# Ranks in the lists of a graph network's first GAT pass, later tables in rank order, and layer ends worked off by groups of 14 blocks

## What is computed

```python
h = jnp.maximum(_layernorm(x, axis=-1), 0.0)
x = x + _L0_gnn_ref(h, src, dst, 12500)                 # cosine attention over src
h = jnp.maximum(_layernorm(x, axis=-1), 0.0)
x = x + _L1_gnn_ref(h, edge_index, ...)                 # two GATs, each: segment softmax, bias, norm, ELU
h = jnp.maximum(_layernorm(x, axis=-1), 0.0)
x = x + _L2_gnn_ref(h, edge_index, W, b)                # GCN: D^-1/2 A D^-1/2 (h W) + b, ReLU
h = jnp.maximum(_layernorm(x, axis=-1), 0.0)
x = x + _L3_gnn_ref(h, r, a, Wa_w, ..., src, dst, edge_type_4)   # gates and attention by edge type
```

## Time and profile before

| | |
|---|---|
| median of 3 runs | 14001.26 us (13983.39 to 14005.41) |
| the profiled execution: its time, its span | 13982.26 us, 13980.5 us |
| POOL busy | 9215.6 us (66%), 9579 instructions |
| DVE busy | 6105.5 us (44%) |
| ACT, PE busy | 1970.1 us (14%), 1991.1 us (14%) |
| DMA, mean over the span | 43 GB/s |

### The profile page before, as it was taken

One profiled execution on the slowest core, in us unless ns is written; L12 is line 12 of the kernel. 1 busy time (PEld: TensorE's weight loads), 2 busy tenths in 40 slices (PEclk: granted clock), 3 DMA queues, 4 the chain that ended last, 5 costly groups with the idle time before them and its releaser, 6 DMA issues. The chain is left out here.

```text
span 13980.5 us, 109214 instructions
## 1 busy us (share of the span) xinstructions
PE 1991.1 (14%) x7172; PEld 1317.2 (9%) x7172; DVE 6105.5 (44%) x20057; ACT 1970.1 (14%) x6083; POOL 9215.6 (66%) x9579
## 2 busy tenths in 40 slices
PE   8720000000010000001000000100000053333334
PEld 6620000000000000001000000000000032222223
DVE  9981233333333333344333334411111157777775
ACT  0000000010011111101000000100000034444443
POOL 0026576776757777775777777477777747777775
PEclk9755555555555555555555555555555555555555
DMA  0001233334211111111111111011111144444442
GB/s 10 0 27 25 34 27 27 28 28 27 27 22 30 30 30 30 30 29 20 28 28 27 28 28 27 16 27 27 27 27 27 26 177 108 107 108 107 107 104 64
DMA packets 971030, 594.72 MB, mean 43 GB/s; under 512 B 713282, under 2 KB 815699, under 8 KB 970561
## 3 DMA queue, kind: packets, MB, share of 16 engines
q0 software_dynamic: 338528, 472.50, 19.1%
q1 hardware_dynamic: 632411, 121.34, 4.9%
HBM read 507.46 MB, written 85.57 MB: 42 GB/s over the span
## 5 line engine op out<-in xcount | busy, mean ns | idle before, releaser
L926 POOL DMA_INDIRECT got<-gat_tab,list x3472 | 3283.3, 946 | 1116.4 <-issue 1006.8
L926 POOL DMA_INDIRECT got<-rel_tab,list x1736 | 1741.0, 1003 | 644.0 <-issue 472.3
L926 POOL DMA_INDIRECT got<-h_tab,list x1736 | 1661.1, 957 | 713.6 <-issue 519.4
L926 POOL DMA_INDIRECT got<-gcn_tab,list x1736 | 1637.6, 943 | 555.0 <-issue 523.0
L1310 DVE COPY e<-top 128x4 f32 (+1 forms) x920 | 149.5, 163 | 2617.9 <-DMA got<-gat_tab,list 2060.1
L1213 PE MATMUL p_t<-ident,staged 128*128 128x128 f32 x147 | 69.4, 472 | 7277.3 <-ACT staged L1229 7266.4
L1416 DVE TENSOR_REDUCE chunk_sum<-got 128x64 f32<-128x256 f32 (+1 forms) x460 | 253.4, 551 | 1771.0 <-DMA got<-gcn_tab,list 1724.9
L1012 DVE TENSOR_TENSOR prod<-got,h 128x256 f32<-128x256 f32 (+1 forms) x460 | 190.1, 413 | 1402.2 <-DMA got<-h_tab,list 1302.3
L1380 ACT ACTIVATE p<-e 128x20 f32<-128x20 f32 (+3 forms) x920 | 195.6, 213 | 4104.2 <-DVE e L1329 3572.0
L533 POOL DMA_INDIRECT info_tab<-info,rank_i x98 | 125.1, 1277 | 976.7 <-DVEq L511 947.1
L1981 PE MATMUL p_gate<-got,ident 128*128 128x256 f32 (+1 forms) x920 | 539.5, 689 | 1483.0 <-DVE gate L1818 1482.4
(11 more groups left out here) (353 smaller groups left out, 7994.4 us busy)
## 6 DMA issues: line engine op xcount, KB each, us to landing
own<-own_tab SPq DMA_DIRECT2D x460, 160.5 KB, 2.4
got<-gat_tab,list POOLq DMA_INDIRECT x3472
got<-h_tab,list POOLq DMA_INDIRECT x1736
got<-gcn_tab,list POOLq DMA_INDIRECT x1736
got<-rel_tab,list POOLq DMA_INDIRECT x1736
own_tab<-own SPq DMA_DIRECT2D x98, 160.5 KB, 2.6
list<-chunks_dst SPq DMA_DIRECT2D x612, 4.0 KB
chunks_src<-rows_src SPq DMA_DIRECT2D x505, 4.5 KB
```

What stands on the lines that cost most here:

```text
L926: pool.indirect_dma_start(r.got[:, q, j, :], None, table, at(r.lists[s][:, c, j:j + 1]))\
```

## The change

The first table is still written by node number. Its rows grow from 72 to 77 values: own scores, and as the last one four times the row's rank (`number_rows` fills it). In the first GAT pass (`relabel`), which loads all columns of the lists, DVE builds from each gathered row's last value the chunk's list anew (`ranks`): ranks, and ranks times four plus type. ACT writes the turn's four new lists to a second list table, `chunks_rank`, with one DMA, and DVE's next turn waits for that DMA. All later passes read `chunks_rank`, and so their tables can lie in rank order and are written with plain DMAs.

The part of two slots now runs ahead of the part of four in the two GAT and the GCN passes. In the part of four, DVE's and ACT's loops over turns are cut at the ends of seven groups of 14 blocks (the ends are in the new row 9 of `row_i`). After the turns of group g, DVE runs `close(g)`: what `gat_close`, `open_layer` and `gcn_close` did, on 14 blocks (896 columns). After the turns of group g + 1 it takes TensorE's products of group g (`finish(g)`), and ACT writes them to the next table; after the last group nothing lies in between. In the GCN pass TensorE and ACT make the rows of `rel_tab` and `own_tab` of a group from its `close` on, 14 blocks one after the other: three matmuls of 321 columns for each block (the third adds the bias), four activations and two DMAs. SP's loop and POOL's loop over the turns stay whole. The whole-layer stages between these passes are gone, but for the first `project_and_spread` and `gat_open`; `gcn_norm` runs ahead of the first GAT, and the tables' last 128 rows (for empty slots) are written in `load_weights`.

```diff
-def load_lists(nc, sp, lists, part, r, i):
+def load_lists(nc, sp, lists, part, r, i, tab, columns):
...
+def group_turns(eng, lists, g):
+    return (eng.value_load(lists.row_i[0:1, 9, bass.ds(g, 1)], min_val=0, max_val=CHUNKS // RING - 2),
+            eng.value_load(lists.row_i[0:1, 9, bass.ds(g + 1, 1)], min_val=1, max_val=CHUNKS // RING - 2))
...
+                def ranks(q):
+                    chunk = r.lists[q // PER_STAGE][:, q % PER_STAGE, :]
+                    if q == 0:
+                        dve.wait_ge(again_out, i * 16 + 16)
+                    ts.add(nc.vector.scalar_tensor_tensor(out=type_of[:, :], in0=chunk[:, 0:S], scalar=-4.0,
+                                                          in1=chunk[:, SLOTS:SLOTS + S], op0=ALU.mult, op1=ALU.add))
+                    ts.add(nc.vector.tensor_scalar(again[:, q, 0:S], r.got[:, q, :, RW - 1], 0.25, None, ALU.mult))
+                    ts.wait()
+                    dve.sem_inc(r.list_used[q // PER_STAGE], 1)
+                    ts.add(nc.vector.tensor_tensor(again[:, q, SLOTS:SLOTS + S], r.got[:, q, :, RW - 1], type_of[:, :],
+                                                   ALU.add))
...
+            def close(g):
+                blocks = bass.ds(g * GROUP, GROUP)
...
+                ch.link(tt(Y[:, :, :], Y[:, :, :], vec(after.bias), ALU.add))
...
+                dve.wait_ge(std_ready, g * NORMS + 1)
...
+                tt(Y[:, :, :], Y[:, :, :], vec(after.shift), ALU.add).then_inc(y_ready, 1)
+                dve.wait_ge(ex_ready, g + 1)
...
+            def group(g):
+                t0, t1 = group_turns(dve, lists, g)
+                one_block(nc, dve)
+                with dve.Fori(t0, t1) as i:
+                    turn(i)
+
+            group(0)
+            close(0)
+            with dve.Fori(1, TURNS) as g:
+                group(g)
+                finish(g - 1)
+                close(g)
+            finish(TURNS - 1)
...
+                if relabel:
+                    act.wait_ge(e_ready, i * RING + RING)
+                    act.dma_start(k.rank_tab[bass.ds(i * RING + part.base, RING), :, 0:SLOTS + S]
+                                  .rearrange("a p c -> p a c"), again[:, :, :]).then_inc(again_out, 16)
...
+            def store(g):
+                blocks = bass.ds(g * GROUP, GROUP)
+                act.wait_ge(finished, g + 1)
+                act.sem_inc(r.tick, 1)
+                act.dma_start(by_rank(after.table)[:, blocks, :], after.state[:, blocks, 0:after.columns])\
+                    .then_inc(stored, 16)
...
-def gcn_edges(nc, k, part, state, table):
+def gcn_edges(nc, k, part, state, table, after):
...
+                    for j in range(GROUP):
...
+                        act.wait_ge(made, g * GROUP + j + 1)
+                        act.wait_ge(out[w], g * 64 + (32 * (j // HELD) + 32))
...
+                        act.dma_start(by_rank(k.rel_tab)[:, blk, :], rows[w][:, :, :].rearrange("p t c -> p (t c)")
+                                      .unsqueeze(1)).then_inc(out[w], 16)
+                        act.dma_start(k.own_tab[blk].rearrange("a p c -> p (a c)"), own[w][:, :]).then_inc(out[w], 16)
...
-def gat_close(nc, k, heads, c, state, bias, gain, shift, y, x_add):
...
-def gcn_close(nc, k, state, dis, bias, x):
...
-def rel_tables(nc, k, h):
...
+    short_first = PARTS[::-1]
```

More of the change, by code:

```diff
@@ L876, in _, with ring_buffers @@
                 dve.wait_ge(copied[j], TURNS * len(parts))
-def ring_buffers(m, part, width, stages=STAGES):
+def ring_buffers(m, part, width, stages=STAGES, columns=None):
     S = part.slots
@@ L883, in ring_buffers @@
     r.per_stage = RING // stages
-    r.lists = [m.sb(f"list{s}", [P, r.per_stage, S], I32) for s in range(stages)]
+    r.columns = columns or S
+    r.lists = [m.sb(f"list{s}", [P, r.per_stage, r.columns], I32) for s in range(stages)]
     r.meta = m.sb("meta", [1, RING], I32)
@@ L992, in _ @@
                 with sp.Fori(0, n) as i:
-                    load_lists(nc, sp, lists, part, r, i)
+                    load_lists(nc, sp, lists, part, r, i, lists.chunk_tab, part.slots)
         @block.gpsimd
@@ L1272, in gat_edges @@
     S = part.slots
+    lists = k.at_dst
     with ExitStack() as ctx:
         m = Mem(nc, ctx)
-        r = ring_buffers(m, part, W)
+        RW = table.shape[1]
+        r = ring_buffers(m, part, RW, columns=SLOTS + S if relabel else S)
         e = m.sb("e", [P, 2, S + 1, heads])
@@ new lines, in finish @@
+            def finish(g):
+                blocks = bass.ds(g * GROUP, GROUP)
+                dve.sem_clear(close_step)
+                ch = Chain(dve, close_step)
+                dve.wait_ge(made, g + 1)
+                after.rows(dve, ch, blocks, p_o[:, :, 0:GROUP // 2, 0:after.wide].rearrange("p y j w -> p j y w"))
+                dve.sem_inc(finished, 1)
+            if not after:
+                one_block(nc, dve)
+                with dve.Fori(0, n) as i:
+                    turn(i)
+                return
@@ L1377, in _, with turn @@
-            with act.Fori(0, n) as i:
+            n = turns(act, lists, part)
+            def turn(i):
                 for q in range(RING):
@@ new lines, in store, with group @@
+            def store(g):
+                blocks = bass.ds(g * GROUP, GROUP)
+                act.wait_ge(finished, g + 1)
+                act.sem_inc(r.tick, 1)
+                act.dma_start(by_rank(after.table)[:, blocks, :], after.state[:, blocks, 0:after.columns])\
+                    .then_inc(stored, 16)
+            if not after:
+                one_block(nc, act)
+                with act.Fori(0, n) as i:
+                    turn(i)
+            else:
+                def group(g):
+                    t0, t1 = group_turns(act, lists, g)
+                    with act.Fori(t0, t1) as i:
+                        turn(i)
+                group(0)
+                close(0)
+                with act.Fori(1, TURNS) as g:
+                    group(g)
+                    close(g)
+                    store(g - 1)
+                store(TURNS - 1)
+                act.wait_ge(stored, 16 * TURNS)
@@ L1418, in _, with close @@
                     dve.sem_inc(r.got_free[q], 1)
-                    ts.link(nc.vector.tensor_tensor(own, own, chunk_sum[:, :], ALU.add))
+                    ts.link(nc.vector.tensor_tensor(own_row, own_row, chunk_sum[:, :], ALU.add))
+            if not after:
+                one_block(nc, dve)
+                with dve.Fori(0, n) as i:
+                    turn(i)
+                return
+            def close(g):
+                blocks = bass.ds(g * GROUP, GROUP)
+                dve.sem_clear(close_step)
+                ch = Chain(dve, close_step)
+                flat = lambda t: t.rearrange("p b d -> p (b d)")
+                xb = x[:, blocks, :]
+                ch.link(nc.vector.tensor_tensor(Y[:, :, :], state[:, blocks, :], bc(dis[:, blocks].unsqueeze(2), full),
+                                                ALU.mult))
+                ch.link(nc.vector.tensor_tensor(Y[:, :, :], Y[:, :, :], bc(bias[:, :].unsqueeze(1), full), ALU.add))
+                ch.link(nc.vector.scalar_tensor_tensor(out=flat(xb), in0=flat(Y[:, :, :]), scalar=0.0, in1=flat(xb),
+                                                       op0=ALU.max, op1=ALU.add))
+                dve.wait_ge(taken, g * GROUP + 2)
+                dve.sem_inc(r.tick, 1)
+                relu_norm(nc, dve, ch, xb, hg[:, :, :], sq[:, :, :], st, full, var_ready, std_ready, g + 1)
+                ch.link(nc.vector.tensor_copy(h[:, blocks, :], hg[:, :, :]))
+                dve.sem_inc(h_ready, 1)
@@ L1422, in gat_open, with number_rows, _ @@
+def number_rows(nc, k, column):
+    with ExitStack() as ctx:
+        numbered = Mem(nc, ctx).sem("numbered")
+        block = ctx.enter_context(nc.Block())
+        @block.vector
+        def _(dve):
+            nc.vector.tensor_scalar(column, k.node_i[:, :], 4.0, None, ALU.mult).then_inc(numbered, 1)
+            dve.wait_ge(numbered, 1)
 def gat_open(nc, k, heads, c, state, own_dst, top):
@@ new lines, in other_layers, with third_rows @@
+            after = After(vec(2), 1, D, x, k.w_gcn, D, D, gcn_state, k.gcn_tab)
+            def third_rows(dve, ch, blocks, made):
+                pairs = lambda t: t.rearrange("p (j y) w -> p j y w", y=2)
+                ch.link(nc.vector.tensor_tensor(pairs(gcn_state[:, blocks, :]), made,
+                                                pairs(bc(dis[:, blocks].unsqueeze(2), [P, GROUP, D])), ALU.mult))
+            after.rows = third_rows
+            for part in short_first:
+                gat_edges(nc, k, part, 1, D, state2, top2, own_dst2, k.gat2_tab, k.rank_tab, False,
+                          after if part.writes else None)
@@ L2200, in other_layers @@
+        for part in short_first:
+            gcn_edges(nc, k, part, gcn_state, k.gcn_tab,
+                      (x, h, dis, k.vec["L2_gnn_b"]) if part.writes else None)
```

495 lines of the change are left out of this document (235 added, 260 removed).

## The result

The changed kernel takes 13649.5 us, the median of four runs (13647.8 to 13653.8). The kernel before takes 14003.3 beside it. The ratio is 0.9751, with a 95% interval from 0.9734 to 0.9767, so it is faster by 2.5%. The forecast was 13660. The profiled execution took 13649.2 us with a span of 13647.4; that of before 13982.3 and 13980.5.

A forecast was written before the change was run, and what follows sets the result against it. POOL's gathers were taken to bound the passes, DVE not. Gaps giving back 599 us, less 233 lost inside passes and 25 for lists, `number_rows` and contention, make 341 us less: 13660 as a median (13641 against the profiled execution), range 13540 to 13830.

The forecast's parts named there:

- The room of 16 gathers: At inner group ends POOL goes on with 16 gathers of the next turn until e + 20.3, while DVE closes.
- The sum inside the passes: POOL's lost time at six inner group ends per pass: 85, 118 and 30 us, together 233 us.
- rivals 1 and 2: 1: ring covers nothing, no change, 13990 to 14030, 0.10 with nearby cases; 2: covers more, half the loss, 13540, 0.06.
- DVE's way from `close` to its next turn: After each close, DVE loads the group's bounds (1.5 us) and starts the turn (2.5 us).
- The port: Two-input DVE instructions hold POOL's gathers: GAT ring filling some 7 us slower, hidden; GCN about 5 us per close, not 1.7.
- the 2.3 us that the prediction named as a sign: Beside the closes, POOL's gathers were to take about 2.3 us in the changed kernel's timeline.
- behind 1.13 us instructions a gather then takes the time of two: In the closes, a gather waits for two DVE instructions: 2.3 us instead of 1.25.
- The new lists: Making lists costs 17 us in the first GAT's two-slot turns, `number_rows` and port contention 8 more: 25 us together.
- the 17 us for the part of two slots: In 13 two-slot turns of the first GAT, DVE goes from about 9.2 to 11.3 us: 17 us.
- Rival 3: Writing the new lists holds up DVE in the first GAT; at landings of 16.5 us the kernel takes 14420; chance 0.04.
- The gaps: POOL's idle between passes, 776.1 us, shrinks to 45.5, 51.2 and 80.0 us, so 599 us come back.
- 14 blocks at the dearer of TensorE ... 3.0 us: GCN-to-relational gap: each block takes TensorE's three matmuls at 1.0 us, 3.0 us, against ACT's 2.4; 42 us in all.

The follow-up runs named there:

- the long closes: Six more two-input VectorE operations (6.9 us) in each close, against the changed kernel with a ring of eight chunks instead of four: 13523.9 us.
- The longer closes: Two kernels, each close of the changed kernel longer by six VectorE operations, with two inputs or with one: 13747.3 and 13742.8 us.

## Why the prediction was right, and where its steps were off

**The room of 16 gathers** carried the sum, and it holds. The sum inside the passes was 233 us; the stops measure 215.5. Counted from e, the end of a group's 16th gather of its last turn, over the five last stops of each pass, POOL came back at about e + 35.3, e + 40.9 and e + 23.5, where the working has 34.4, 39.9 and 22.0. The ring was full at e + 20.3 to 21.4 in the GATs and at e + 20.0 in the GCN, where it has 20.3. The ring of eight chunks took all 18 stops away, and the long closes brought back those, and only those, that the room of 32 gathers did not cover. This speaks against rivals 1 and 2: the ring does not cover nothing, and it covers no more than was counted.

**Two small errors pulled against each other.** DVE's way from `close` to its next turn was sized at 1.5 + 2.5 = 4.0 us; it takes 4.5 in the GCN, 4.6 to 4.9 in the first GAT and 5.0 to 5.6 in the second, while from SP's issue of the list to the gather it is 2.7 us for 3.1. The port was said to slow the filling of the ring in the GATs by some 7 us and to cost the GCN 3.3 us a close. It slows it by 0.3 to 1.4 us in the GATs, and in the GCN the filling takes 20.0 us, as without a close. No gather beside a close took the 2.3 us that the prediction named as a sign: the longest is 1.82 us in the GATs and 1.02 in the GCN. Of the 17 us too many in the 233, 11.5 are the GCN's. The step that failed is "behind 1.13 us instructions a gather then takes the time of two": the earlier trace rows has instructions of 6.83 us back to back, and it doesn't carry over to a chain of short ones with 0.03 us between, where most gathers are not held. The longer closes put it at 0.2 to 0.4 us for an operation of 1.09.

**The new lists** were put at 25 us with `number_rows` and contention. The measured counterpart is about 44: 36 in the passes beside the stops, and 7.5 ahead of the first GAT. Of these 7.5, 3.4 stand already at the end of the cosine pass, which the change does not touch, and another 3.4 lie between the layer norm and the first transposes (1.5 us before, 4.9 now), where `gcn_norm` and `number_rows` stand. Of the 17 us for the part of two slots 8.0 came. The other places were not named: 6.4 us at the changes of parts, and the rest of the 36, some 22 us, nearly all in the four-slot parts. The run with no new lists takes back only 11.9 us in all, the 8.2 of the two-slot part and about 1 us a stop in the first GAT. The changes of parts take 13.6 to 14.3 us in it and with all closes behind the pass too, so they belong to neither. The 22 us belong to the closes for the most part: with all closes behind the pass the four-slot parts of the GATs take 2038.9 and 2038.4 us; in the changed kernel, less their stops, 2132.2 - 82.9 = 2049.3 and 2162.6 - 114.1 = 2048.5. Rival 3 did not come near: without the write nothing is faster (13622.5 for 13622).

**The gaps.** 45.3 and 48.5 us against 45.5 and 51.2: right within 3 us. The GCN's is 93.4 against 80.0, and the step that failed is "14 blocks at the dearer of TensorE ... 3.0 us". The groups of the changed kernel from 11052 to 11146 us, for 14 blocks:

```profile
L1682 PE MATMUL p_w<-own_bias,ones 1*128 1x321 f32 x28 | 20.1, 817 | 0.0
L1680 PE MATMUL p_s<-w_src,hT 64*128 64x321 f32 x28 | 20.1, 819 | 1.1 <-ACT hT L1695 1.1
L1681 PE MATMUL p_w<-w_own,hT 64*128 64x321 f32 x28 | 17.8, 738 | 0.0
```

and one block in the timeline:

```profile
11073.73 0.39 ACT L1701 ACTIVATE rows<-p_s 128x260 f32<-128x260 f32 x1 [4.12 <-PE p_w L1682]
...
11077.34 1.43 PE L1680 MATMUL p_s<-w_src,hT 64*128 64x321 f32 x2
11077.45 0.39 ACT L1701 ACTIVATE rows<-p_s 128x260 f32<-128x260 f32 x1 [2.42 <-PE p_w L1682]
...
11081.14 0.90 PE L1680 MATMUL p_s<-w_src,hT 64*128 64x321 f32 x1
11081.25 0.39 ACT L1701 ACTIVATE rows<-p_s 128x260 f32<-128x260 f32 x1 [2.50 <-PE p_w L1682]
```

A product takes 1.3 to 1.4 us (17.8 / 14 and 20.1 / 14), and the block 3.8: 14 x 0.8 = 11 of the missing 13 us. The 1.0 us came from the busy sum of the earlier trace rows, 97.5 us for 98 products. There 196 records of 787 ns would sum to 154, so they overlapped one another, and a busy sum counts overlapping records once. In the chain of a block they hardly overlap. The clock is not the cause. In the changed kernel the granted clock is the low one of 1.2 GHz, 0.50, from 11052 to 11125 us; in the old stage it is 0.56 on average from 11262 to 11440, with short spells at 2.4 GHz. But from 11290 to 11300 it is 0.50 there too, and four records, two products, take 1.94 us:

```profile
11295.58 1.94 PE L1593 MATMUL p_s<-w_src,hT 64*128 64x321 f32 x4
```

Why products overlap in the old stage and not in this order stays open; that the bias product uses the same half of the rows as the one ahead of it was tried and is not the reason by itself. The rest of the estimate for this gap held: from the last store's issue (11125.3) to the gather 20.3 us, for 20.5.

**The sum.** Too much given back in the GCN's gap, 13 us, and too little in the second GAT's, 3; 19 too little counted for lists and contention; 17 too much for the stops, and the 3.5 from the relational pass on, which no term stands for. It came out 8 us from the measured 333 because these errors have both signs, which is luck; the two terms that decide, the cover and the gaps, were each right within 8% and 2%.

## What to carry to other kernels

When work is moved into a loop that feeds on a ring of buffers, its price is the time that the ring's consumer is away, from its last release to its next one, less the time the producer needs to fill the ring. Count both from the same point, and if the stop is shorter than one ring's worth, a ring twice as deep removes it. Take the time of a step in a chain from the distance of two like starts in the timeline and not from a busy sum, which hides overlap; and before you blame the releaser that the profile names, compare the idle time with that of a place where it can't be waited for.

## What the runs showed of the hardware

- At the granted clock of 0.50 a product with a single row (1x321) takes TensorE 817 ns a record, as much as one with 64 rows (738 to 819). Cut to 65 columns it takes 441, and the next product starts 0.61 us behind it instead of 1.36. Here the columns set the time, not the rows.
- Six VectorE operations of 1.09 us with two inputs made POOL fill its ring 1.1 to 2.6 us later than six of the same length with one input. In the GCN's close of the changed kernel, where at most three two-input operations follow one another, the filling is not slowed (20.0 us). Beside operations of 6.83 us an indirect DMA takes 6.85 us instead of 0.95.
- A loop body of VectorE twice as long (eight chunks instead of four) ran without a visible cost: the four-slot part of the GCN took 2036.9 us, with four chunks and no stops 2037.1.
